# Chunked state-space layer on one core: the decay factors made in the prologue and brought in by repeating transfers, and two matmul groups in another order

## The reference, cut to what matters

```python
Ac = jnp.transpose(chunk(Adt), (0, 3, 1, 2))
A_cumsum = jnp.cumsum(Ac, axis=-1)
L = jnp.exp(segment_sum(Ac))
Gm = jnp.einsum('bcihn,bcjhn->bhcij', C, B)
Y_diag = jnp.einsum('bhcij,bcjhd->bcihd', Gm * L, xs)
...
state_decay = jnp.exp(A_cumsum)
Y_off = jnp.einsum('bckhn,bchdn,bhck->bckhd', C, states, state_decay)
y = (Y_diag + Y_off).reshape(b, l + pad, NH, HD) + D_res
```

## Time and profile before

| | us |
|---|---|
| median of 3 runs | 2206.22 |
| the runs | 2206.22, 2206.24, 2197.03 |
| the profiled execution | 2204.8 |
| its span, first to last instruction | 2203.1 |
| PE busy | 2061.4 (94%) |
| DVE busy | 1593.6 (72%) |
| ACT busy | 964.0 (44%) |
| POOL busy | 465.2 (21%) |

### The profile page before, as it was taken

How to read it: one execution, slowest core, us unless ns; L and a number is a source line. 1 busy time by engine, 2 the same in 40 slices (tenths; PEclk the granted TensorE clock), 3 DMA queues, 4 the chain that set the end, 5 groups by cost and what they waited for, 6 DMA issues and landing times.

```text
span 2203.1 us, 26984 instructions
## 1 busy us (share of the span) xinstructions
PE 2061.4 (94%) x10056; PEld 1383.9 (63%) x10056; DVE 1593.6 (72%) x2303; ACT 964.0 (44%) x1290; POOL 465.2 (21%) x385
## 2 busy tenths in 40 slices
PE   6799957999999999999999999999999999999987
PEld 4344425676767676766676666666666666666654
DVE  6443423586868686868687868798887879797965
ACT  2100003655555545454545445454544545455531
POOL 1100023222222222222222222222121222222200
PEclk9799988999999999999999999999999999999998
DMA  5000003213131312121212231211212121212110
GB/s 196 29 15 0 1 19 100 59 35 104 35 104 35 99 40 94 44 94 45 87 46 91 57 114 48 81 57 59 75 59 80 54 80 54 85 54 80 54 44 20
DMA packets 67361, 139.14 MB, mean 63 GB/s; under 512 B 11280, under 2 KB 16528, under 8 KB 66720
## 3 DMA queue, kind: packets, MB, share of 16 engines
q1 hardware_dynamic: 67232, 137.42, 19.4%
HBM read 127.69 MB, written 9.70 MB: 62 GB/s over the span
## 4 chain that ended last, share of the span: by engine, by line
PE 66%; issue 6%; DVE 6%; ACT 5%; DMA 2%; POOL 1%; SPq 0%; POOLq 0%; ACTq 0%; DVEq 0%
PE bank L710 31%; PE bank L809 18%; PE bank L726 4%; PE bank L739 3%; PE bank L761 3%; DVE conv L1046 2%; PE bank L768 2%; ACT wos L926 2%; PE bank L751 2%; DVE conv L1050 2%; DMA wxs<-wp 2%; ACT L906 1%; ACT conv L877 1%; PE bank L792 1%; ACT M L906 1%
## 5 line engine op out<-in xcount | busy, mean ns | idle before, releaser
L710 PE MATMUL bank<-xnp,wxp 128*128 128x512 f32 x3456 | 883.7, 408 | 43.5 <-POOLq L1018 30.0
L710 PEld LDWEIGHTS bank<-xnp,wxp 128*128 128x128 f32 x3456 | 650.8, 192 | 199.5 <-POOLq L1018 30.9
L981 POOL TENSOR_TENSOR wxp<-wxs,wxp 128x512 fp32r<-128x512 f32 x288 | 392.4, 1367 | 1097.8 <-ACT wxp L870 1097.7
L809 PE MATMUL bank<-wos,gT 128*128 128x512 f32 x1024 | 453.2, 596 | 2.6 <-DVE gT L1126 2.6
L1046 DVE SCALAR_TENSOR_TENSOR conv<-bank,cws,conv 128x509 f32<-128x509 f32 (+2 forms) x480 | 357.9, 746 | 31.1 <-ACT conv L877 19.8
L809 PEld LDWEIGHTS bank<-wos,gT 128*128 128x128 f32 x1024 | 191.0, 192 | 218.9 <-issue 215.9
L877 ACT ACTIVATE conv<-bank,cbs,cws 128x512 f32<-128x512 f32 x160 | 123.9, 775 | 310.3 <-PE bank L710 310.3
L870 ACT ACTIVATE wxp<-wxs 128x512 fp32r<-128x512 f32 x288 | 179.2, 622 | 62.4 <-DMA wxs<-wp 44.9
L1153 DVE SCALAR_TENSOR_TENSOR M<-M,gb 128x1024 f32<-128x1024 f32 x128 | 176.4, 1378 | 7.5 <-DVE gb L1145 0.5
L901 ACT ACTIVATE xT<-conv 128x512 f32<-128x512 f32 x160 | 100.1, 625 | 186.4 <-DVE conv L1050 110.2
L885 ACT ACTIVATE gT<-bank 128x512 f32<-128x512 f32 x128 | 76.3, 596 | 224.2 <-PE bank L710 223.5
(11 more groups left out here) (133 smaller groups left out, 2128.1 us busy)
## 6 DMA issues: line engine op xcount, KB each, us to landing
wxs<-wp SPq DMA_DIRECT2D x288, 256.0 KB, 2.7
wos<-wout SPq DMA_DIRECT2D x64, 512.0 KB, 5.3
state_scratch<-S SPq DMA_DIRECT2D x8, 512.0 KB, 2.9
S<-state_scratch SPq DMA_DIRECT2D x8, 512.0 KB, 3.6
w1s<-w SPq DMA_DIRECT2D x1, 3584.0 KB, 14.3
w2s<-w SPq DMA_DIRECT2D x2, 1792.0 KB, 20.7
out<-acc SPq DMA_DIRECT2D x8, 256.0 KB, 3.2
tab_scratch<-tabs SPq DMA_DIRECT2D x2, 768.0 KB, 4.8
```

The source lines that it names most:

```text
L710: last = pe.matmul(bank(k), wxp[:, k % 2, a, kk, :], xnp[:, half, b, kk, :], start=kk == 0 and a + b == 0, stop=kk == KT - 1 and a == 1)
L809: last = pe.matmul(Y[:, 512:512 + HID], gT[u % 2][:, t, tokens(q)], wos[:, t, :], start=t == 0, stop=t == XT - 1)
L981: pool.tensor_tensor(wxp[:, k % 2, 1], wxs[:, k % 2], wxp[:, k % 2, 0], ALU.subtract).then_inc(w_lo, 1)
```

## The change

The exponential of the cumulative sums is taken once, in the prologue: ACT turns all of `csT` (128x1024) into `v`, and SP writes it to a new scratch tensor in memory, `ecs_scratch`, 128 heads by 1024 tokens, 512 KB. POOL's split of `csT` now waits for that exponential. In the scan, `spread`, `exp_c` and the matrix `pick` are gone. Instead SP issues two transfers per cell, `load_ecs(q+2)`, into one of two buffers of `ecs`: each fills 64 partitions, and every one of them reads the same eight rows of 512 bytes. So a cell moves 1024 pieces of 512 bytes, 512 KB.

On PE `from_state(q+1)` moves up behind tile 3, and `segment_b(q+1)` moves down behind tile 4. On SP `load_row(q+2)`, which stood ahead of the load that follows tile 4, moves behind all tile loads of the cell, and `load_ecs(q+2)` follows it.

```diff
@@ prologue, sync
+            sp.wait_ge(s_ecs, 1)
+            sp.dma_start(ecs_dram, v[:].rearrange("p t h -> p (t h)")).then_inc(s_spill, 16)
             sp.wait_ge(s_seg, 2 * PARTS - 1)
             sp.dma_start(cs_dram.rearrange("m h t -> h m t"), csb[:]).then_inc(s_spill, 16)
...
@@ prologue, scalar
+            act.wait_ge(s_csT, 2)
+            act.activation(v[:].rearrange("p t h -> p (t h)"), csT[:].rearrange("p t c -> p (t c)"),
+                           ACT.Exp).then_inc(s_ecs, 1)
...
@@ scan, sync
+            def load_ecs(q):
+                if q < CELLS:
+                    _, half, g, c = place(q)
+                    t0 = (half * CH + c) * P
+                    sp.wait_ge(u1_d, done(q - 1))
+                    for e in range(2):
+                        rows = ecs_dram[g * HG:(g + 1) * HG, t0:t0 + P].rearrange("(t e) i -> e t i", e=2)[e]
+                        sp.dma_start(ecs[e * HD:(e + 1) * HD, q % 2], bc(rows, 0, [HD, XT, P])).then_inc(d_ecs[q % 2], 16)
...
             load_row(0)
+            load_ecs(0)
+            load_ecs(1)
             load_out(0)
...
                 for i, k in enumerate(tiles_of(q)):
-                    if i == 3:
-                        load_row(q + 2)
                     load_tile(k + 2)
-                if not tiles_of(q):
-                    load_row(q + 2)
+                load_row(q + 2)
+                load_ecs(q + 2)
...
@@ scan, tensor
                 if more:
                     segment_a(q + 1)
-                    spread(q + 1)
                 for k in ks[2:3]:
                     project(k)
                 if more:
-                    segment_b(q + 1)
+                    from_state(q + 1)
                 for k in ks[3:4]:
                     project(k)
                 if more:
-                    from_state(q + 1)
+                    segment_b(q + 1)
                     gram(q + 1)
...
@@ scan, scalar
                 if more:
                     exp_a(q + 1)
-                    exp_c(q + 1)
                 square(q)
...
@@ scan, gpsimd
-            pool.memset(pick[:], 0.0).then_inc(built, 1)
...
-                pool.affine_select(out=pick[:], in_=pick[:], compare_op=ALU.not_equal, fill=1.0, base=-PAIRS - m * HG,
-                                   pattern=[[-2, XT], [-1, 2], [0, HD]], channel_multiplier=1).then_inc(stage, 1)
...
@@ scan, vector, decay_off
-                dve.wait_ge(e_c, done(q + 1))
+                dve.wait_ge(d_ecs[q % 2], 32 * (q // 2 + 1))
```

More of the change, by code:

```diff
@@ L172, in prologue @@
         s_seg = sem("p_seg")
+        s_ecs = sem("p_ecs")
         s_split = sem("p_split")
@@ L285, in tables @@
                 if half:
-                    act.wait_ge(s_spill, 16 * (1 + half))
+                    act.wait_ge(s_spill, 16 * (2 + half))
                 for k, src in ((1, av), (2, tot)):
@@ L368, in tables @@
                 if half:
-                    dve.wait_ge(s_spill, 16 * (1 + half))
+                    dve.wait_ge(s_spill, 16 * (2 + half))
                 dve.wait_ge(s_tab, 4 * half + 2)
@@ L503, in scan @@
 def scan(nc, sb, sem, banks, wxs, d_w, xnp, acc, ident, upper, epsc, wp, wout, cws, cbs, nws, dch, d_const,
-         cs_dram, tab_dram, rest_dram, state_dram, out):
+         cs_dram, ecs_dram, tab_dram, rest_dram, state_dram, out):
     with ExitStack() as ctx:
@@ L520, in scan @@
         xdec = sb(ctx, "xdec", [P, GC])
-        ecs = sb(ctx, "ecs", [P, GC])
+        ecs = sb(ctx, "ecs", [P, 2, XT, P])
         ya = sb(ctx, "ya", [P, XT, P])
@@ L533, in scan @@
         d_out, d_acc_in = sem("d_out"), sem("d_acc_in")
+        d_ecs = [sem(f"d_ecs{p}") for p in range(2)]
         d_tab = [sem(f"d_tab{p}") for p in range(2)]
@@ L605, in _ @@
         def _(sp):
-            sp.wait_ge(built, 11)
+            sp.wait_ge(built, 10)
             def load_tile(k):
@@ L696, in _ @@
         def _(pe):
-            for s in (t_mm, yo_mm, st_mm, xt_mm, yd_mm, ec_mm, sa_mm, sb_mm, g_mm, o_mm, q_mm):
+            for s in (t_mm, yo_mm, st_mm, xt_mm, yd_mm, sa_mm, sb_mm, g_mm, o_mm, q_mm):
                 pe.sem_inc(s, CREDIT)
@@ L723, in from_state @@
                     pe.wait_ge(s_add, done(q))
-                pe.wait_ge(e_c, done(q + 1))
+                pe.wait_ge(x_dt, done(q + 1))
+                pe.wait_ge(x_dec, done(q + 1))
                 for t in range(XT):
@@ L746, in turn_x @@
                 pe.wait_ge(u1_d, done(q))
-                pe.wait_ge(e_c, done(q))
+                pe.wait_ge(x_dec, done(q))
                 if c == 0:
@@ L784, in segment_b @@
                 segment(q, 1)
-            def spread(q):
-                u, _, _, c = place(q)
-                pe.wait_ge(x_dt, done(q + 1))
-                pe.wait_ge(x_dec, done(q + 1))
-                for t in range(XT):
-                    last = pe.matmul(Z[:, t * P:(t + 1) * P], pick[:, t, :], segl[:, u % 2, c], start=True, stop=True)
-                last.then_inc(ec_mm, 1)
             def gram(q):
@@ L825, in _ @@
                     segment_b(0)
-                if k == 16:
-                    spread(0)
                 project(k)
@@ L861, in _ @@
         def _(act):
-            for s in (w_hi, tap_d, silu_d, z_d, e_a, e_b, e_c, y_sq, wo_n):
+            for s in (w_hi, tap_d, silu_d, z_d, e_a, e_b, y_sq, wo_n):
                 act.sem_inc(s, CREDIT)
@@ L910, in exp_b @@
                 act.activation(M[:, HG // 2:].rearrange("p h t -> p (h t)"), X[:], ACT.Exp).then_inc(e_b, 1)
-            def exp_c(q):
-                act.wait_ge(ec_mm, done(q + 1))
-                act.wait_ge(u1_d, done(q))
-                act.activation(ecs[:], Z[:], ACT.Exp).then_inc(e_c, 1)
             def square(q):
@@ L937, in _ @@
                     silu(k - 1)
-            exp_c(0)
             for n in range(PIECES):
```

33 lines of the change are left out of this document (17 added, 16 removed).

## The result

| | before | after |
|---|---|---|
| median, us | 2205.46 | 2258.2 |
| the runs | 2197.03 to 2206.24 | 2253.61 to 2262.35 |
| the profiled execution's span | 2203.1 | 2260.6 |

The ratio is 1.0248, interval 1.0212 to 1.0283: the changed kernel is 2.5% slower, where 2.9% faster was forecast.

The account below looks back on a forecast made before the run. PE was taken as the bound, busy 1627 of 1670 us. Gains of 14.4 + 3.9 + 32.0 + 8.5 + 5.7 less 0.5 at the start, 64.0 us, gave 2142 us; forecast band 2128 to 2152, range 2128 to 2205.

Parts of the forecast that it names:

- The transfers: Factor loads on the DMA queue: 2.4 us a cell, hidden; up to 2.9 us costs nothing at unit starts.
- t: DMA time of a cell's factors: 2.4 us taken; 3.2 or 7.0 by the other two prices.
- t - 1.3: Loss in us at each of 14 unit starts with dear factors; change slower than before above t = 5.4 us.
- four `spread`s: PE's chain: removing `spread` saves 0.45 us a cell, 14.4 us in the first half, 3.9 in the second.
- slow tiles: Tiles at low clock behind PE's wait for `exp_a`: six of 14 become normal, 8.5 us gained.
- The start: Prologue: 4.3 us less POOL work against 4.8 us of two cells' factors, net 0.5 us lost.
- The last unit: Last unit, without tiles: 4.9 us from `segment_a` to `project_out` become 3.0 in three cells, 5.7 us gained.
- Dear pieces: Rival: factors at t = 7.0 us delay unit starts and the start by 89 us, 2231 us; chance 0.15.
- `exp_b` too late: Rival: tile 5 waits 1 us in 30 cells, 2172 us; within a shared chance of 0.25.
- DVE takes the bound: Rival: second-half convolutions in c0 and c1 give back 16.2 and 4.6 us, 2163; within a shared 0.25.
- It does not do what it says: Rival: wait before `segment_b` isn't from ACT; only `spread`, start and end gain, 23.5 us, 2182; chance 0.08.
- What would show it: Signs: no PE wait before c0's second segment half; DMA queue share up 7%, or 20% if dear.

Follow-up runs that it names:

- onerow: The changed kernel, but each factor transfer reads one and the same 512-byte row 512 times: 2271.01 us, ratio 1.0310 to before.
- pad: The changed kernel with each row of `ecs_scratch` 512 bytes longer, so a partition's eight rows lie 9216 bytes apart: 2132.12 us, ratio 0.9683 to before.
- pad128: The changed kernel with each row of `ecs_scratch` 128 bytes longer, so a partition's eight rows lie 8448 bytes apart: 2152.04 us, ratio 0.9766 to before.
- contig: The changed kernel with a partition's eight rows side by side in `ecs_scratch`, read as one 4 KB piece: 2133.11 us, ratio 0.9682 to before.
- oldorder: The kernel with 4 KB pieces side by side, but `segment_b` and `from_state` back in their old places: 2186.55 us, ratio 0.9931 to before.
- order: The kernel before with `segment_b` behind tile 4 and `from_state`, `load_row` behind the tile loads; `spread` and `exp_c` stay: 2175.25 us, ratio 0.9874.

## Why the prediction was wrong

**The step that failed** is the price in "The transfers": 2.4 us of DMA time a cell, taken from the 768-byte rows, instead of the row with repeated reads, 7.0. The runs showed 8.8 us in its place. This is by the text's own formula, in which `wos` starts t - 1.1 us late: tile 3's weights, behind `wos`, were issued 7.7 us late at the unit start shown, which makes t = 8.8 us, 138 ns a piece. The medians of landing agree: `wos` lands 13.1 - 5.3 = 7.8 us later than in before. Even the dear end, 113 ns by the clock on the wall, was too low, and it was the one row with this kind of source. The reason given against it, eight rows for the engines to spread over, is what onerow and pad refute: eight rows at this distance were nearly as dear as one (8.6 and 9.7 us), and 9216 bytes apart they were cheap.

**The mechanism** behind the price stood. With t = 8.8 the formula gives t - 1.3 = 7.5 us for each unit start; measured were 8.5 in the first half and 7.5 in the second. For pad128 t is 4.0 (`wos` lands at 8.2 instead of 5.3 us, t = 2.9 + 1.1), where the prediction has 2163; measured 2152. That is no strong support: its 21 us leave out the 1.4 us of slow clock that t - 1.3 has in it (with them it would be some 40), and the waits for POOL at pad128's unit starts are uneven, from none to 3.3 us. One thing in it wasn't foreseen: SP doesn't run ahead of the data. It is held in the issues of `wos` (9.42 us), so everything behind them is late even as an issue. Nor was unit 7, where SP waits for `out` to land behind the factors; "a transfer other than those of the unit's end is held up" was named as a sign of being wrong, and it came true there and at the start.

**Term by term**, with the price taken out (contig against before, from the table of units):

- In a unit of the first half four `spread`s, one wait and its share of slow tiles were 1.8 + 15.8 / 7 + 8.5 / 14 = 4.7 us; measured 112.56 - 107.48 = 5.1. In the second half 0.55 + 2.3 + 0.6 = 3.5; measured 3.7. Both held, if a little low.
- The start: 0.5 us lost was forecast. In contig PE begins tile 2 at 348.20 instead of 352.00, 3.8 us gained; in after it loses 7.7. That is the price again: the head of the queue carries two cells' factors.
- The last unit: 5.7 us forecast, 9.5 measured in contig (90.8 to 81.3). The size was off by 3.8 us. oldorder gains 2.8 of the 9.5 (88.0), and the order on top of it 6.7, but order without the transfers loses 4.2 us there (95.0): the new order pays there only without `exp_c`. What the 3.8 us are, no run separates.
- The sum: 64 us forecast, 2142; 2133 measured where the transfers are cheap, within the forecast's own range (2128 to 2152).

**The rivals.** "Dear pieces" came true, with 0.15, and at a higher price than its own: 2231 against 2258. "`exp_b` too late" fell: the 17 waits for POOL are the start and before tile 3 of a cell; none stands before tile 5. "DVE takes the bound" fell too, though DVE is close: PE's waits for its convolutions went from 3.9 us to 10.0 in after and 9.9 in contig, longest 1.2, as forecast (1.1). "It does not do what it says" fell with the wait for `exp_a`.

**What would show it** was right in the waits and wrong in the share of the DMA queue. It named 7% more for the cheap price and 20% for the dear one. The share rose from 19.4% to 26.0% at the dear price, and to 26.8% in contig at the cheap one. The share was low, 29% and 55%, just while the dear factors held up what stood behind them, so it doesn't show such a hold-up. Nor is the price by busy share, 38 ns a piece in after ((26.0% of 2260.6 x 16 us, less 19.4% of 2203.1 x 16) / 67728 packets added), a sign of what it costs on the wall: it is about the 37 ns that the prediction took, while by the clock on the wall they are 138.

In weighing, the text had one row of the same kind as the new work and one of another kind but with more packets, and took the second. Chances of 0.78 and 0.15 did not follow from that. And the range, which reached 2205, left out the case with the widest span of price.

## What to carry to other kernels

A price for a new transfer is taken from the row whose source is read in the same way (repeated or not, at which distance), by the clock on the wall from issue to landing, not by size alone and not by busy share. Where many partitions read the same few small rows, it is worth trying to pad the rows or to lay them side by side in one piece: here, at a distance of 8192 bytes, 512 bytes more a row were worth 126 us. A transfer that is asked for a whole cell later should be issued where nothing urgent stands behind it; that was worth 114 us by itself. And a wait that is measured behind some work grows when that work is taken away: `spread` gained nothing in c0 as long as PE waited for `exp_a` there.

## What the runs showed of the hardware

- A transfer of 256 KB in pieces of 512 bytes lands after 9.7 us when all pieces are one row, 8.6 from eight rows 8192 bytes apart, 5.0 at 8448, 4.4 at 9216, and 4.1 from 512 different rows 8192 apart. Pieces of 4 KB read by 64 partitions each, 4.2. Least, median and longest of the factors' transfers in after, then in contig:

```profile
DMA to landing us min/median/max: 6.4/8.6/16.2
```
```profile
DMA to landing us min/median/max: 3.3/4.2/6.3
```

- An issue can hold SP when the queue is far behind. Four issues of `wos` took 1.75 us with little ahead of them, and 3.5 to 10.9 us behind the dear factors, a single one up to 4.3 (least, median and longest issue of after in ns):

```profile
L651 SPq DMA_DIRECT2D wos<-wout x64: 342/1937/4305, 337.6 to 2179.0; - x64
```

- Idle times of PE of 3.6 to 7.7 us are followed by a tile of 4.4 to 5.5 us instead of 2.8 to 3.1, at a mean granted clock of 0.56 in the one shown; behind one of 1.98 us (unit 7) the tile took 3.07. Over a quarter of what a late transfer costs here is that tile: 2.3 us beside 6.1 us of wait.
